# Learning loop of a convolution-attention hybrid: another order of work on four engines, one gradient in pairs of batches, tanh in SBUF

## The reference

```python
def _mlp(params, h):
    for w1, w2 in params:
        h = h + jax.nn.gelu(h @ w1) @ w2
    return h
def assoc_loss(p, k, v):
    return jnp.mean((_mlp(p, k) - v) ** 2)
def step(carry, x_t):
    params, mom = carry
    k = _l2norm(x_t @ Wk); v = x_t @ Wv
    ...
    g = grad(assoc_loss)(params, k, v)
    new_mom = eta * mom - lr * g
    new_params = params * (1.0 - forget) + new_mom
    return (new_params, new_mom), None
```

## Time and profile before

| | us |
|---|---|
| median of 3 runs | 1007.38 |
| lowest, highest | 1003.4, 1008.6 |
| the profiled execution | 1005.29 |
| its span, first to last instruction | 1003.5 |

### The profile page before, as it was taken

The page is one execution under the profiler, slowest core; times in us unless marked ns, Lnnn a source line. Parts: engine busy times, 40 slices in busy tenths (PEclk is TensorE's granted clock), DMA queues, the critical chain, the costliest instruction groups (busy, mean ns, idle before and its releaser), DMA issues. The chain is left out here.

```text
span 1003.5 us, 24055 instructions
## 1 busy us (share of the span) xinstructions
PE 754.5 (75%) x7837; PEld 474.5 (47%) x7837; DVE 721.0 (72%) x1821; ACT 615.7 (61%) x1382; POOL 587.0 (58%) x760
## 2 busy tenths in 40 slices
PE   2766888888888888888888859965576521999960
PEld 2453444445444544444444524431165421899950
DVE  2576778778788788887877861569777771677757
ACT  2565777777777777777777723228633320988840
POOL 0045686776777767768677649920006674466660
PEclk9996999999999999999999969977855555999995
DMA  9009999990000000000000015014001112233318
GB/s 227 1 2 173 157 204 159 20 5 0 0 0 0 0 0 0 0 0 0 0 0 0 0 26 145 0 44 143 2 2 38 48 51 62 65 95 89 92 54 251
DMA packets 109052, 54.07 MB, mean 54 GB/s; under 512 B 42688, under 2 KB 100824, under 8 KB 109008
## 3 DMA queue, kind: packets, MB, share of 16 engines
q1 hardware_dynamic: 102624, 43.34, 28.5%
q0 software_dynamic: 4544, 9.38, 2.9%
q10 hardware_dynamic: 1840, 0.79, 0.5%
HBM read 21.49 MB, written 29.44 MB: 51 GB/s over the span
## 5 line engine op out<-in xcount | busy, mean ns | idle before, releaser
L528 DVE SCALAR_TENSOR_TENSOR l_m<-l_m,l_eta,lp_g 128x256 f32<-128x256 f32 x512 | 219.3, 475 | 46.4 <-PE lp_g L641 26.0
L383 POOL TENSOR_TENSOR s_w<-l_kw,l_m 128x512 f32<-128x512 f32 x192 | 238.4, 1281 | 12.2 <-DVE l_m L528 12.2
L476 ACT ACTIVATE l_kw<-s_w,l_keep_lr 128x256 f32<-128x256 f32 x384 | 171.2, 506 | 0.0
L1333 POOL DMA_INDIRECT f_yg<-f_yr,f_xmeta x78 | 78.4, 1005 | 54.5 <-DVE f_yr L1663 41.7
L1328 POOL DMA_INDIRECT f_xg<-f_xrow,f_place x64 | 63.2, 988 | 54.3 <-DVE f_place L1559 35.7
L469 ACT COPY l_wt<-lp_b 128x512 f32<-128x512 f32 x96 | 56.5, 588 | 27.7 <-PE lp_b L634 27.7
L1308 ACT ACTIVATE f_hh<-fp_v,f_bcol 128x256 f32<-128x256 f32 x156 | 61.3, 477 | 12.9 <-DVE f_hs_lo L1654 8.5
L388 POOL TENSOR_TENSOR l_kw<-s_w,l_keep 128x512 f32<-128x512 f32 x64 | 65.1, 1035 | 0.0
L634 PE MATMUL lp_b<-s_cst,s_w 128*128 128x128 f32 x384 | 62.2, 285 | 2.2 <-ACT s_w L515 1.3
L634 PEld LDWEIGHTS lp_b<-s_cst,s_w 128*128 128x128 f32 x384 | 43.3, 142 | 32.2 <-ACT l_wt L469 13.8
L1428 PE MATMUL fp_v<-f_xf,s_w_hi 128*128 128x256 bf16 x312 | 55.5, 280 | 1.4 <-DVE f_xmeta L1643 1.0
(11 more groups left out here) (320 smaller groups left out, 1991.3 us busy)
## 6 DMA issues: line engine op xcount, KB each, us to landing
f_xg<-s_pad SPq DMA_DIRECT2D x1, 17280.0 KB, 107.0
f_xt<-f_xg SPq DMA_DIRECT2D x39, 130.0 KB
r_w<-in_L_ffn_W_dram SPq DMA_DIRECT2D x16, 256.0 KB, 3.2
s_w<-f_yg SPq DMA_DIRECT2D x16, 256.0 KB, 3.7
xs<-in_x_dram SPq DMA_DIRECT2D x8, 256.0 KB, 7.6
t_w<-in_L_ffn_W_dram SPq DMA_DIRECT2D x8, 256.0 KB
out_dram<-s_x SPq DMA_DIRECT2D x8, 256.0 KB, 3.0
s_xsh<-s_xl SPq DMA_DIRECT2D x4, 448.0 KB, 3.5
```

The costliest lines, as they stand in the source:

```text
L383: nc.gpsimd.tensor_tensor(W[k][:, half(h), :], KW[k][:, half(h), :], M[k][:, half(h), :], ALU.add).then_inc(w_ready[k], 1)
L476: m = nc.scalar.mul(KW[k][:, b, :], W[k][:, b, :], keep_lr[:, b:b + 1])
L528: i = nc.vector.scalar_tensor_tensor(out=M[k][:, b, :], in0=M[k][:, b, :], scalar=eta[:, b:b + 1], in1=ps_g[b][:, 0:256], op0=ALU.mult, op ...
L1333: nc.gpsimd.indirect_dma_start(sb["yg"][:, :], bass.IndirectOffsetOnAxis(ap=xmeta[:, j, a, 0:1].bitcast(mybir.dt.int32), axis=0), yr[j % R ...
```

## The change

TensorE, VectorE, ScalarE and GpSimd each get a new order of the same instructions. VectorE's `slope_in` and `slope_out` are split into `cubic` (`u`), `weighted` (`dd`), `bent` (`v`) and `slope` (`gp`), which are placed one by one. The gradient of "20" is made for batches 0 and 1, then for 2 and 3, each with a signal; GpSimd's adds and keeps are called by half, and ScalarE's keeps one batch at a time with signals for each half. Tanh goes to a tile `th` in SBUF. GpSimd's wait for W20 ahead of `keep` is no longer there. The diff, cut to its core:

```diff
 GpSimd
 forward:
-                    if grads:
-                        pool.wait_ge(kept["11"], p * 2 + 2)
-                        add(p, "11", G11)
...
                         nc.gpsimd.tensor_copy(keep_lr[:, :], step_of(t, "coef")[:, 4:9]).then_inc(lr_in, 1)
+                    if grads:
+                        add(p, "11", G11, 1)
+                    if steps:
                         nc.gpsimd.tensor_tensor(sk...)
+                        pool.wait_ge(lr_in, t + 1)
+                        nc.gpsimd.tensor_tensor(keep...)
                         nc.gpsimd.tensor_copy(kx...)
-                        pool.wait_ge(lr_in, t + 1)
-                        pool.wait_ge(w_ready["20"], t * 2 + 2)
...
-                        nc.gpsimd.tensor_tensor(keep...)
+                        pool.wait_ge(keep_in, t + 1)
+                        keep_of(t, "11", 0)
...
                         scaled(kk, keep).then_inc(kk_ready, 1)
-                        keep_of(t, "11")
                         if grads:
                             pool.wait_ge(mom_ready, mom(p, G10, 1))
                         nc.gpsimd.tensor_copy(eta...)
-                        nc.gpsimd.tensor_copy(kc...)
                         pool.wait_ge(eta_in, t + 1)
                         scaled(ke, eta).then_inc(ke_ready, 1)
                     if grads:
-                        add(p, "10", G10)
+                        add(p, "10", G10, 0)
+                    if steps:
+                        keep_of(t, "11", 1)
+                    if grads:
+                        add(p, "10", G10, 1)
+                    if steps:
+                        nc.gpsimd.tensor_copy(kc...)
 backward:
-                    add(t, "21", G21)
+                    add(t, "21", G21, 0)
+                    add(t, "11", G11, 0)
+                    add(t, "21", G21, 1)
 ScalarE
-                    nc.scalar.activation(p[:, 256:512], u[l][:, :], ACT.Tanh, scale=GELU_C).then_inc(tanh_ready[l], 1)
+                    nc.scalar.activation(th[l][:, :], u[l][:, :], ACT.Tanh, scale=GELU_C).then_inc(tanh_ready[l], 1)
...
 new order, forward:  hidden 0, wt 21 first half, square 0, gf0, keep 21 batch 0, wt 21 second half,
                      keep 21 batch 1, keep 20 batch 0, h1f, tanh 0, wt 11 first half
 new order, backward: hidden 1, wt 20 second half, gf1, square 1, keep 20 batch 1, wt 20 first half, tanh 1, dpf,
                      wt 11 second half, daf, keep 10 batches 0 and 1, keep 21 batch 2, dh1f,
                      keep 10 batch 2, 21 batch 3, 20 batch 2, 10 batch 3, 20 batch 3
 VectorE, forward:
-                        momentum(p, "20", G20, range(B))
+                        momentum(p, "20", D20A, (0, 1))
+                        momentum(p, "20", D20B, (2, 3))
                         update(p, "20", G20)
-                        slope_in(t, 0, ps_a)
+                        cubic(t, 0, ps_a)
+                        weighted(t, 0)
                         h1
+                        momentum(p, "10", D10, (0,))
                         hv
-                        slope_out(t, 0, ps_a)
-                        momentum(p, "10", G10, (0, 1))
-                        slope_in(t, 1, ps_b)
-                        momentum(p, "10", G10, (2, 3))
+                        momentum(p, "10", D10, (1, 2, 3))
+                        bent(t, 0)
+                        cubic(t, 1, ps_b)
 backward:
                     dp
-                    slope_out(t, 1, ps_b)
-                    momentum(t, "21", G21, (0, 1))
+                    weighted(t, 1)
+                    bent(t, 1)
+                    slope(t, 1)
+                    momentum(t, "21", D21, (0,))
                     slope_times(t, 1, ps_a, DG1)
-                    momentum(t, "21", G21, (2, 3))
-                    momentum(t, "11", G11, (0, 1))
+                    momentum(t, "21", D21, (1, 2, 3))
                     dh1
-                    momentum(t, "11", G11, (2, 3))
+                    slope(t, 0)
+                    momentum(t, "11", D11, range(B))
                     slope_times(t, 0, ps_b, DG0)
 TensorE, forward:
+                        pe.wait_ge(mom_ready, mom(p, G11, 0))
+                        grad_2(g[0], dh1, (0, 1))
                         pe.wait_ge(mom_ready, mom(p, G11, 1))
-                        grad_2(g[0], dh1)
+                        grad_2(g[0], dh1, (2, 3))
...
                         down(ps_h, gf[0], W["20"])
+                        pe.wait_ge(sq_ready, t * 2 + 1)
+                        pe.wait_ge(u_ready[0], t + 1)
+                        pe.wait_ge(w_ready["11"], t * 2 + 1)
+                        turn_w("11", 0)
                         pe.wait_ge(chain, t * 6 + K_H1)
                         turn(h1, 128)
-                        pe.wait_ge(chain, t * 6 + K_HV)
-                        turn_w("20", 1)
...
                         up(ps_b, h1f, W["11"])
+                        pe.wait_ge(chain, t * 6 + K_HV)
+                        turn_w("20", 1)
 backward:
                     turn(g[1], 256)
-                    pe.wait_ge(slope_ready[0], t * 2 + 2)
-                    turn_w("11", 0)
+                    pe.wait_ge(wt_ready, t * 6 + X11A)
+                    turn_w("20", 0)
...
                     down(ps_h, gf[1], W["21"])
-                    pe.wait_ge(wt_ready, t * 6 + X11A)
-                    turn_w("20", 0)
...
                     turn(da[1], 256)
-                    pe.wait_ge(mom_ready, mom(t, G21, 1))
-                    grad_1(h1, da[1])
-                    pe.wait_ge(wt_ready, t * 6 + X11B)
-                    pe.wait_ge(gf_ready, t * 6 + TDA1)
-                    down(ps_h, daf, WT["11"])
                     if not last:
...
                         up(ps_a, kk, W["10"], stop=False)
+                    pe.wait_ge(wt_ready, t * 6 + X11B)
+                    pe.wait_ge(gf_ready, t * 6 + TDA1)
+                    down(ps_h, daf, WT["11"])
+                    pe.wait_ge(mom_ready, mom(t, G21, 1))
+                    grad_1(h1, da[1])
```

More of the change, by code:

```diff
@@ L310, in learn @@
         h1f, dpf, dh1f = (buf(n, [128, 128]) for n in ("h1f", "dpf", "dh1f"))
-        q, u, dd, v, gp = ([buf(f"{n}{l}", [128, 256]) for l in range(2)] for n in ("q", "u", "dd", "v", "gp"))
+        q, u, dd, v, gp, th = ([buf(f"{n}{l}", [128, 256]) for l in range(2)] for n in ("q", "u", "dd", "v", "gp", "th"))
         def bank(name, n=1):
@@ L331, in learn @@
         G21, G11, G20, G10 = range(4)
-        X21A, X21B, X20B, X11A, X20A, X11B = range(1, 7)
+        D21, D11, D20A, D20B, D10 = range(1, 6)
+        X21A, X21B, X11A, X20B, X20A, X11B = range(1, 7)
         K_H1, K_HV, K_DP, K_DA1, K_DH1, K_DA0 = range(1, 7)
@@ L377, in per_batch, with add, keep_of @@
                     return x[:, :].rearrange("p (b a) -> p b a", a=1).to_broadcast([128, B, n])
[L379 to L390, removed]
+                def add(t, k, n, h):
+                    pool.wait_ge(kept[k], t * 2 + h + 1)
+                    pool.wait_ge(mom_ready, mom(t, n, h))
+                    nc.gpsimd.tensor_tensor(W[k][:, half(h), :], KW[k][:, half(h), :], M[k][:, half(h), :], ALU.add).then_inc(w_ready[k], 1)
+                def keep_of(t, k, h):
+                    pool.wait_ge(w_ready[k], t * 2 + h + 1)
+                    nc.gpsimd.tensor_tensor(KW[k][:, half(h), :], W[k][:, half(h), :],
+                                            keep[:, half(h)].rearrange("p (b a) -> p b a", a=1).to_broadcast([128, 2, 256]),
+                                            ALU.mult).then_inc(kept[k], 1)
                 def scaled(dst, gate):
@@ L451, in square, with tanh @@
                     nc.scalar.activation(q[l][:, :], p[:, 0:256], ACT.Square, scale=GELU_A ** 0.5).then_inc(sq_ready, 1)
-                def tanh(t, l, p):
+                def tanh(t, l):
                     act.wait_ge(u_ready[l], t + 1)
-                    nc.scalar.activation(p[:, 256:512], u[l][:, :], ACT.Tanh, scale=GELU_C).then_inc(tanh_ready[l], 1)
+                    nc.scalar.activation(th[l][:, :], u[l][:, :], ACT.Tanh, scale=GELU_C).then_inc(tanh_ready[l], 1)
                 def feature(t, n, dst, width, scale=None):
@@ L469, in wt, with keep_of @@
                     nc.scalar.copy(flat(WT[k][:, half(h), :]), wt_bank(k, h)).then_inc(wt_ready, 1)
-                def keep_of(t, k, batches):
-                    act.wait_ge(w_ready[k], t * 2 + 2)
+                def keep_of(t, k, b):
+                    act.wait_ge(w_ready[k], t * 2 + (2 if k == "20" else b // 2 + 1))
                     act.wait_ge(lr_in, t + 1)
-                    for b in batches:
-                        m = nc.scalar.mul(KW[k][:, b, :], W[k][:, b, :], keep_lr[:, b:b + 1])
-                    if b == B - 1:
+                    m = nc.scalar.mul(KW[k][:, b, :], W[k][:, b, :], keep_lr[:, b:b + 1])
+                    if b == B - 1 or (b == 1 and k != "20"):
                         m.then_inc(kept[k], 1)
@@ L521, in _, with momentum @@
```

(19 more changed lines are left out.)

57 lines of the change are left out of this document (32 added, 25 removed).

## The result

The changed kernel takes 1057.38 us (median of 4 runs, 1056.02 to 1057.97) where the kernel before, with the runs beside it, takes 1005.39 (4 runs, 1003.23 to 1008.6): a ratio of 1.053, 95% interval 1.050 to 1.055. The forecast was 1055, slower. The profiled execution took 1056.02 us, its span is 1054.2.

What follows compares the result with a forecast made beforehand. A chain through several engines, filling TensorE, was taken to bound the 15.55 us step. Reordering −0.71 and SBUF meetings +2.28 gave 17.12 a step, +49 us over 31 steps, perhaps 1 more outside: 1055 us, range 1000 to 1092.

Steps and rivals of the forecast that it cites:

- Items 1 to 4: W20's paired gradient, moved turns, ScalarE's order, `down` of `daf` ahead of "11"'s gradient: −0.22, −0.14, −0.18, −0.45 us a step.
- Item 2: Weight turns moved on TensorE: turn of `h1` to `up` −0.14 us; the next turn, of `g1`, unchanged (±0).
- Item 5: `da0` behind all four momenta of "11" on VectorE: `down` of `daf` to `sk` 3.47 us instead of 3.19, +0.28.
- Item 6: W20's update and `dd0` meet GpSimd's adds: `h1` 1.0 us late if the add is first, otherwise 0.5; taken as +0.75.
- Item 7: `dd1`, `v1`, `gp1` each get in only between two GpSimd instructions, delaying `da1`: +1.53 us a step.
- Item 8: `v0` and `gp0` fall into GpSimd's waits for the momenta of "10" and "11": 0 us.
- The order holds: Rival: the fused form does not stop or finds gaps, update first; −0.71 us a step, 983 us; chance 0.18.
- Few meetings: Rival: half of the 2.28 us is spared or only the update stops; 1005 to 1018 us; chance 0.13.
- The clock falls too: Rival: TensorE's idle time halves its clock, +2 to +3 us a step more; 1117 to 1148 us; chance 0.07.
- The sum over the shared resource: GpSimd's 11.57 us, the update's 1.14 and six times 0.34: 14.75 us a step in which one engine excludes the other.

Runs made afterwards that it cites:

- run 7: The kernel of run 5 with the first two momenta of "20" waiting for all 16 matmuls of their gradient: 1002.26 us, ratio 0.997.
- run 3: The changed kernel with GpSimd waiting for W20 ahead of its second add of "11": 1045.84 us, ratio 1.043.
- run 5: The kernel of run 1 with GpSimd's copy `kc` behind the second add of "10" and ScalarE's first keeps later: 987.78 us, ratio 0.982.
- run 2: The changed kernel with the second input of `dd1`, `v1` and `gp1` read from an unused PSUM tile: 1015.41 us, ratio 1.013.
- run 6: The kernel of run 5 with `dd0` moved behind `h1` on VectorE: 1001.99 us, ratio 0.998.
- run 1: The changed kernel with GpSimd reordered to keep clear of VectorE's two-SBUF-input instructions, and some ScalarE keeps moved: 998.53 us, ratio 0.994.
- run 4: The kernel before the change with tanh written to SBUF and nothing else changed: 1021.95 us, ratio 1.018.

## Why the prediction was right

The forecast and its mechanism held: 1055 for 1057, a step of 17.12 for 17.23. By its own steps:

- **Items 1 to 4** came nearly as laid out. The momenta of "20" start 0.33 behind `da0` (270.65; forecast 0.34; run 7 shows that this is the pairs' doing). `down` of `daf` starts 0.99 after the turn (0.98). `up` of `dpf` starts 1.32 after `dp` (1.40). `up` of `h1f` starts 0.78 after its turn (0.71).
- **Item 2's "±0"** held for the turn of `g1` (1.14 behind `up`, forecast 1.15), but from that turn to the `down` of `gf1` it takes 1.13, not 1.00. With 0.07 more for `h1f`, `h1` to `dp` is 4.20, not 4.02. The moved turn of W20 gives ScalarE a copy that stands ahead of `gf1`'s, and TensorE waits 0.26 us for that one (278.92).
- **Item 5, the price of a late `da0`,** was too low by 0.24: `down` of `daf` to `sk` is 3.71 (284.66 less a step of 17.27 gives 267.39, and `sk` at 271.10), not 3.47. It counted the momenta of "11" and then `sk`, but not the second half of the gradient of "20", which waits for the last of these momenta and stands ahead of `sk` on TensorE: `da0` to `sk` is 0.78, not 0.53. This did not lengthen the step: W20's update, for which `down` of `gf0` waited 0.76 us, follows from `da0` through the momenta of "20" and not from `sk`.
- **Item 6, +0.75 between 0.5 and 1.0.** The add came 3.55 after the first momentum of "11" (forecast 3.61), the update 3.65 (3.70): the add first, by 0.10 us. From `da0` to `h1` it takes 5.21 us; 4.95 with the update first (run 3, `da0` at 300.66) and 4.37 with neither held long (run 5). So 0.84 as it went and 0.58 the other way round, where 1.0 and 0.5 were forecast. The +0.75 was the middle of two branches that the sum could not tell apart; that it lies 0.09 from what came is partly luck.
- **Item 7, +1.53.** Counted from `h1`: `dd1` at 4.47 (4.29), `v1` at 5.59 (5.55), `gp1` at 6.94 (7.0), `da1` at 7.67 (7.65). With the trio free, `da1` starts 2.03 us after `dp` (run 2) in place of 3.47: +1.44.
- **Item 8** held: `v0` (277.56) and `gp0` (268.30) took 0.42.

Items 6 and 7 come to 2.28 us, as in the forecast's sum, with +0.09 and −0.09 in its two terms. Along the chain of the step shown, 17.27 us and so 0.15 over the forecast, `h1` to `dp` is longer by 0.18 (item 2), `da0` to `h1` by 0.15 (5.21 for 5.06, which is 0.53 to `sk`, 2.95 to `down`, 0.83 to `h1` and the 0.75), and `dp` to `da1` shorter by 0.16 (3.47 for 3.63). So the mechanism was right and its terms were near, but the total is closer than they are, because their errors partly cancel; that part is luck. The forecast's last 1 us, for the first forward pass and the tail, had the wrong sign (−2.7 and +1.4).

The doubt that the prediction left, whether the fused form stops, is settled by run 2 against the changed kernel: 0.41 to 0.42 with one PSUM operand, 1.02 and 1.31 with two SBUF ones. (from which the prediction took the standstill of a third form, give a duration alone; the trace has GpSimd on an instruction of 1.16 us beside it, from 642.90 on.) The rule of the Trainium skill, "SBUF — State Buffer", section "Who interferes with whom", which makes no exception for it, agrees with these rows, and with `sk`'s 1.43 us for the block on GpSimd's side.

*The rivals.* "The order holds" fell for the kernel as it stands, but its working was sound: with the meetings taken away (run 5) the step is 15.09, where it forecast 14.84, and the kernel is 1.8% faster than the one before. "Few meetings" is ruled out by the update, `dd1` and `v1`. "The clock falls too" is ruled out by 1.00 in a step in which TensorE stood idle for 1.40 and 0.76 us and was busy for 13.81 of 17.27.

The sum over the shared resource, 14.75 us a step in which one of the two engines keeps the other out, says what is left: run 5's 15.09 is 0.34 above it, so in this order little more is to be had unless work leaves GpSimd or an operand goes back to PSUM. That is an estimate, worked out from the kernel before; no run here tried it.

## What to carry to other kernels

When an operand moves from PSUM to SBUF, or a wait of GpSimd goes, list every VectorE instruction that reads two SBUF tensors and lay GpSimd's row beside it: a meeting in which GpSimd is first costs VectorE most of what is left of GpSimd's instruction, whatever the VectorE instruction's own length (here 1.01 of 1.16 us for the update, 0.60 of 0.73 for `dd1`, 0.89 of 1.03 for `v1`). A wait on GpSimd that carries no data may be what keeps the engines apart; here, ordering GpSimd's queue (and a few keeps of ScalarE's) turned 5% slower into 2% faster without changing a single operation. Before moving even a free-looking instruction, look at what stands behind it in its queue (run 6: 14 us lost for 0.4 us of instruction).

## What the runs showed of the hardware that was not expected

- *The block works on tiny instructions too.* `keep_lr`, a GpSimd copy of 128 x 5 elements, takes 0.18 us alone (272.15 in the changed kernel) and 1.20 behind the update (272.88 in run 1).
- *A small lead decides.* 0.10 us of lead made the update 1.01 us longer. The copy ahead of the add, `keep_lr`, takes 0.18 us, more than the lead; that such a copy can turn the order was not tried.
- *Tanh to SBUF takes longer than to PSUM.* The 128 x 256 tanh has a median of 393 ns in the kernel before, with PSUM as its target, and of 419 in run 4, with SBUF. In the loop this lies off the chain.
- *A single stall in the first pass through the loop's code.* In runs 1, 5 and 7 TensorE waited 2.69, 1.80 and 2.07 us in the first iteration for nothing that the profile shows; in the kernel before it waited 0.72 there, in the changed kernel and in run 6 not at all. Run 1, at the stall:

```profile
98.80 1.33 PE L664 MATMUL lp_g<-l_dh,l_g 32*128 32x128 f32 x9 [2.69 <-issue]
```

The first step of run 1 takes 20.8 us from `dp` to `dp` (89.3 to 110.1), 5.4 more than a later one. The wait is half of that; behind it the granted clock was 0.50 for 5 us (98.8 to 103.8), the lower of its two levels, 1.2 GHz, and 0.82 for the next 5, where it had been 1.00 before (89.3 to 98.8), with TensorE idle for the 2.69 us of the wait just ahead of the fall. The steps of 15.37, 15.09 and 15.48 us given for runs 1, 5 and 7 are of later ones. Why the wait comes in some orders and not in others was not tried, and stays open.
